# Softmax attention on one core: values projected for two groups of heads at once, and the loop over groups written out

## What is computed

```
xq = (x @ wq + bq).reshape(S, 16, 128)        # 16 query heads
xk = (x @ wk + bk).reshape(S, 4, 128)         # 4 groups share a key head ...
xv = (x @ wv + bv).reshape(S, 4, 128)         # ... and a value head
for group g, query head h in g (4 of them):
    attn = softmax(xq[:, h] / sqrt(128) @ xk[:, g].T)     # 1024 x 1024
    out[:, h] = attn @ xv[:, g]
x = x_in + out.reshape(S, 2048) @ wo + bo
```

## Time and profile before

| | before |
|---|---|
| median of three runs | 1137.98 us |
| the profiled execution, its own time | 1133.82 us |
| its span | 1132.0 us |
| mean granted TensorE clock | 0.974 |
| attention phase in it | from about 16 to 623 us |
| busy: TensorE, VectorE, ScalarE, GpSimd | 92%, 67%, 53%, 50% |

### The profile page before, as it was taken

The page is one execution under the profiler, slowest core; times in us unless marked ns, Lnnn a source line. Parts: engine busy times, 40 slices in busy tenths (PEclk is TensorE's granted clock), DMA queues, the critical chain, the costliest instruction groups (busy, mean ns, idle before and its releaser), DMA issues. The chain is left out here.

```text
span 1132.0 us, 18077 instructions
## 1 busy us (share of the span) xinstructions
PE 1045.5 (92%) x6180; PEld 879.3 (78%) x6180; DVE 763.1 (67%) x1344; ACT 599.5 (53%) x1059; POOL 562.3 (50%) x408
## 2 busy tenths in 40 slices
PE   5899999999999999999998989998888887999992
PEld 4788888888887888888887676664666586999992
DVE  4777764777566776657774654466687855788887
ACT  3566653666545666446662433342533235888881
POOL 1574623656335564335650256773324676755553
PEclk9999999999999999999999899999998898999996
DMA  7400440001800672000000236651300266777766
GB/s 198 52 29 1 53 41 3 19 11 33 61 2 2 223 215 84 1 1 1 1 1 1 77 98 208 209 195 56 107 1 5 100 211 214 237 236 234 233 218 212
DMA packets 45641, 109.92 MB, mean 97 GB/s; under 512 B 8519, under 2 KB 26069, under 8 KB 43504
## 3 DMA queue, kind: packets, MB, share of 16 engines
q1 hardware_dynamic: 38640, 95.46, 30.4%
q0 software_dynamic: 6912, 13.30, 3.1%
HBM read 94.27 MB, written 41.29 MB: 120 GB/s over the span
## 5 line engine op out<-in xcount | busy, mean ns | idle before, releaser
L422 POOL TENSOR_TENSOR at_prob<-at_prob,at_inv_sum 128x1024 f32<-128x1024 f32 x128 | 243.8, 1907 | 287.4 <-DVE at_inv_sum L647 287.4
L612 ACT ACTIVATE at_pt_h<-ps 128x512 fp32r<-128x512 f32 x256 | 139.1, 596 | 147.8 <-PE ps L537 147.7
L697 DVE TENSOR_TENSOR at_pt_l<-ps,at_pt_h 128x512 fp32r<-128x512 f32 x256 | 164.5, 684 | 60.6 <-ACT at_pt_h L612 60.5
L686 DVE TENSOR_REDUCE at_neg_max<-ps 128x1 f32<-128x1024 f32 x128 | 156.1, 1219 | 40.4 <-PE ps L41 40.0
L579 ACT ACTIVATE at_prob<-ps,at_neg_max 128x1024 f32<-128x1024 f32 x128 | 143.8, 1123 | 18.4 <-DVE at_neg_max L686 18.4
L537 PE MATMUL ps<-ident,at_prob 128*128 128x128 f32 x1024 | 133.0, 273 | 3.8 <-POOL at_prob L422 3.8
L537 PEld LDWEIGHTS ps<-ident,at_prob 128*128 128x128 f32 x1024 | 119.2, 140 | 20.9 <-POOL at_prob L422 4.7
L2079 POOL DMA_INDIRECT lines<-f_y,f_x_raw x96 | 96.3, 1003 | 71.8 <-ACT f_y L1995 43.7
L39 PE MATMUL ps<-at_k_h,at_q_h 128*128 128x512 f32 x256 | 108.9, 425 | 0.0
L41 PE MATMUL ps<-at_k_h,at_q_l 128*128 128x512 f32 x256 | 100.7, 393 | 0.0
L39 PE MATMUL ps<-at_pt_h,at_v_h 128*128 128x512 f32 x256 | 100.5, 392 | 0.0
(11 more groups left out here) (314 smaller groups left out, 2509.0 us busy)
## 6 DMA issues: line engine op xcount, KB each, us to landing
e_raw<-in_we SPq DMA_DIRECT2D x32, 624.0 KB, 4.1
f_cw_row<-cw SPq DMA_DIRECT2D x32, 512.0 KB, 4.4
slots<-in_empty SPq DMA_DIRECT2D x4, 3456.0 KB, 43.7
f_x_raw<-slots SPq DMA_DIRECT2D x32, 432.0 KB, 4.7
lines<-in_empty SPq DMA_DIRECT2D x3, 2048.0 KB, 32.5
f_e_raw<-in_we SPq DMA_DIRECT2D x32, 128.0 KB, 2.7
at_wq_raw<-in_wq SPq DMA_DIRECT2D x4, 512.0 KB, 3.3
at_wo_raw<-in_wo SPq DMA_DIRECT2D x4, 512.0 KB, 3.3
```

The costliest lines, as they stand in the source:

```text
L422: nc.gpsimd.tensor_tensor(prob[:, t % RING, :], prob[:, t % RING, :], inv_sum[:, t:t + 1].broadcast_to([P, T]), ALU.mult).then_inc(normed, 1)
L612: nc.scalar.activation(pt_h[:, e[1] % PT, :], turned(e[1]), ACT.Copy).then_inc(pt_high, 1)
L686: nc.vector.tensor_reduce(neg_max[:, t:t + 1], slot(n, start), AX.XY, ALU.max, negate=True).then_inc(maxed, 1)
L697: nc.vector.tensor_tensor(pt_l[:, e[1] % PT, :], turned(e[1]), pt_h[:, e[1] % PT, :].bitcast(F32), ALU.subtract).then_inc(pt_split, 1)
```

## The change

The values of two groups are projected together: one stationary token tile against the 256 columns of two value heads, in two jobs `("v", 0)` and `("v", 1)` of four token tiles each. This happens in the opening (groups 0 and 1) and in the change from group 1 to 2 (groups 2 and 3). `v_full`, `v_h` and `v_l` hold two groups. The split of the first group of a pair, `("vs", 0)`, is in the opening or within the change; that of the second, `("vs", 1)`, in the middle of the steady part of groups 0 and 2. The loop over groups is written out on every engine, with constants in place of registers. Keys' and values' weights have buffers, loads and splits of their own. The norm's centred input `xc` lies in the last two slots of `prob`, and its two small buffers are allocated last.

```diff
-    opening = [("k",), ("q", 0), ("v",)] + [("s", s) for s in range(LEAD)] + [("vs",)] + pair("t", 0)
-    steady = []
+    opening = [("k",), ("q", 0), ("v", 0), ("v", 1)] + [("s", s) for s in range(LEAD)] + [("vs", 0)] + pair("t", 0)
+    def steady(g):
+        events = []
...
+            if g % 2 == 0 and s == STEPS // 2:
+                events.append(("vs", 1))
...
-    change = [("k",)] + pair("p", at) + pair("t", at + 4) + [("v",)] + pair("p", at + 2) + pair("t", at + 6)
-    for n in range(3):
-        change += pair("s", 2 * n) + pair("p", at + 4 + 2 * n) + pair("t", at + 8 + 2 * n)
-    change += pair("s", 6) + pair("p", at + 10) + pair("s", 8) + pair("p", at + 12)
-    change += [("vs",)] + pair("s", 10) + [("y", 0)] + pair("t", 0) + [("y", 1)]
+    def change(g):
+        projects = (g + 1) % 2 == 0
+        events = [("k",)] + pair("p", at) + pair("t", at + 4) + [("v", 0)] * projects + pair("p", at + 2) + pair("t", at + 6)
+        events += [("v", 1)] * projects
+        for n in range(3):
+            events += pair("s", 2 * n) + pair("p", at + 4 + 2 * n) + pair("t", at + 8 + 2 * n)
+            events += [("vs", 0)] * (projects and n == 1)
+        events += pair("s", 6) + pair("p", at + 10) + pair("s", 8) + pair("p", at + 12)
+        return events + pair("s", 10) + [("y", 0)] + pair("t", 0) + [("y", 1)]
...
-        norm = Norm(nc, net, "n0", mem, load=True)
+        norm = Norm(nc, net, "n0", mem, load=True, xc=prob[:, RING - 2:, :].rearrange("p r (k d) -> p (r k) d", d=D))
...
             run(-1, opening, 0)
-            with eng.Fori(0, KV - 1) as g:
-                run(g, steady + change, first)
-            run(KV - 1, [e for e in steady if e != ("q", PER)] + closing, first)
+            start = first
+            for g in range(KV):
+                events = steady(g) + (change(g) if g < KV - 1 else closing)
+                run(g, events, start)
+                start += len(jobs_of(events))
...
-                            for i in range(TT):
-                                toks = slice(i * P, (i + 1) * P)
+                            for i in range(TT // 2):
+                                toks = slice((e[1] * TT // 2 + i) * P, (e[1] * TT // 2 + i + 1) * P)
                                 for c in range(DC):
-                                    last = product(nc, slot(n, start)[:, i // 4, (i % 4) * P:(i % 4 + 1) * P], xn_h[:, c, toks],
-                                                   xn_l[:, c, toks], wkv_h[:, 1, c, :], wkv_l[:, 1, c, :], c == 0, c == DC - 1)
+                                    last = product(nc, tokens_of(slot(n, start), i), xn_h[:, c, toks], xn_l[:, c, toks],
+                                                   wv_h[:, c, :], wv_l[:, c, :], c == 0, c == DC - 1)
...
-                            inverts(0 if start == 0 else 3)
-                            if start:
-                                dve.wait_ge(pv_done, LIFT + STEPS * (g + 1))
+                            if start == 0:
+                                inverts(0)
+                            k = e[1]
+                            if k and g:
+                                dve.wait_ge(pv_done, LIFT + STEPS * g)
```

More of the change, by code:

```diff
@@ L273, in jobs_of @@
         return [e for e in events if e[0] in "kvqy" or (e[0] == "s" and e[1] % 2 == 0)]
-    first, lap = len(jobs_of(opening)), len(jobs_of(steady + change))
-    assert lap % 2 == 0
+    first = len(jobs_of(opening))
     with ExitStack() as mem:
@@ L337, in proj_count, with v_high, v_split, keys_ready @@
             if e[0] == "k":
-                return 2 + PROJ * (g + 1) if not (isinstance(g, int) and g < 0) else 1
-            return 2 + PROJ * g + e[1] if not (isinstance(g, int) and g < 0) else 2
+                return 2 + PROJ * (g + 1) if g >= 0 else 1
+            return 2 + PROJ * g + e[1] if g >= 0 else 2
+        def v_high(k):
+            return v_parts, 2 * k + 1
+        def v_split(k):
+            return v_parts, 2 * k + 2
+        def keys_ready(g):
+            return (1, 3, 4, 6)[g]
+        def values_ready(g):
+            return (2, 5)[g // 2]
         def read_of(g, e, nxt):
@@ L345, in read_of @@
             if e[0] == "v":
-                return v_added, own + 1
+                return v_added, own + e[1] + 1
             if e[0] == "s":
@@ L382, in _ @@
                 sp.dma_start(bo[:, :], net.dram["bo"].partition_broadcast(P)).then_inc(consts, 16)
-                with sp.Fori(0, KV - 1) as g:
-                    sp.wait_ge(wo_split, 1 + 4 * g)
+                for g in range(KV - 1):
+                    if g:
+                        sp.wait_ge(wo_split, PER * g)
                     sp.dma_start(wo_raw[:, :, :], net.dram["wo"][g]).then_inc(wo_loaded, 16)
-                    sp.wait_ge(wkv_split, g + 1)
-                    load(g + 1, "kv")
+                    sp.wait_ge(wkv_split, keys_ready(g))
+                    load(g + 1, "k")
+                    if g % 2:
+                        sp.wait_ge(wkv_split, values_ready(g - 1))
+                        load(g + 1, "v")
                     sp.wait_ge(wq_split, 2 * (g + 1))
@@ L457, in _ @@
                         .then_inc(wq_split, 1)
+                pool.wait_ge(w_high, 2 + DC)
+                nc.gpsimd.tensor_tensor(wv_l[:, :, :], wv_raw[:, :, :], wv_h[:, :, :].bitcast(F32), ALU.subtract).then_inc(wkv_split, 1)
                 for t in range(LEAD // 2):
                     normalise(t + 1, t)
-                with pool.Fori(0, KV - 1) as g:
+                for g in range(KV - 1):
                     group(g, range(LEAD // 2, TILES + LEAD // 2))
@@ L466, in run @@
                 def run(g, events, start):
-                    jobs = jobs_of(events)
-                    spots = [n for n, e in enumerate(events) if e in jobs and (e[0] in "kvqy" or e[1] % 2 == 0)]
-                    before = jobs_of(steady + change)[-2:]
+                    spots = [n for n, e in enumerate(events) if jobs_of([e])]
                     n = start - 1
@@ L476, in begin @@
                             sem_, count = read_of(g, events[q], belongs_next(events, q))
[L477 removed]
+                        elif g > 0:
+                            sem_, count = read_of(g - 1, ("y", k), False)
+                        else:
                             return
[L479 to L482 removed]
                         pe.wait_ge(sem_, count)
[L485 to L492 removed]
+                    if g == 0:
+                        pe.wait_ge(exped, LEAD // 2)
                     for place, e in enumerate(events):
@@ L547, in run @@
                             keys = slice(kt * P, (kt + 1) * P)
-                            product(nc, o_bank(u), v_h[:, keys], v_l[:, keys], pt_h[:, e[1] % PT, :], pt_l[:, e[1] % PT, :],
+                            product(nc, o_bank(u), v_h[:, g % 2, keys], v_l[:, g % 2, keys], pt_h[:, e[1] % PT, :], pt_l[:, e[1] % PT, :],
                                     kt == 0, kt == KT - 1).then_inc(pv_done, 1)
@@ L564, in _ @@
                 norm.wait_parts(pe)
-                laps(pe, run)
+                laps(run)
                 bridge(nc, net, 4, 2)
@@ L590, in run @@
                             act.wait_ge(proj_full, count)
-                            if not (isinstance(g, int) and count == 1):
+                            if count > 1:
                                 act.wait_ge(proj_split, count - 1)
@@ L633, in _ @@
                 act.wait_ge(consts, 64)
-                laps(act, run)
+                laps(run)
             @block.vector
@@ L672, in run @@
[L672 to L680 removed]
+                            dve.wait_ge(values_full, own + e[1] + 1)
@@ new lines, in run @@
+                            part = slice(e[1] * BANK, (e[1] + 1) * BANK)
+                            nc.vector.tensor_tensor(v_full[:, :, part].rearrange("p g (i d) -> p i g d", d=DH),
+                                                    slot(n, start).rearrange("p n (i g d) -> p (n i) g d", g=2, d=DH),
+                                                    bv[:, own * DH:(own + 2) * DH].rearrange("p (g d) -> p g d", d=DH).unsqueeze(1)
+                                                    .broadcast_to([P, TT // 2, 2, DH]), ALU.add).then_inc(v_added, 1)
@@ L721, in _ @@
                 nc.vector.tensor_scalar(bq[:, :], bq[:, :], Q_SCALE, None, ALU.mult).then_inc(bq_scaled, 1)
-                laps(dve, run)
+                laps(run)
                 dve.wait_ge(y_added, LIFT + DC * KV)
```

132 lines of the change are left out of this document (63 added, 69 removed).

## The result

The changed kernel takes 1118.87 us (median of four runs, 1118.58 to 1119.49), the kernel before 1137.03 us beside it (four runs, 1133.95 to 1138.25): ratio 0.9858 [0.9842, 0.9874]. In a second series the changed kernel took 1122.21 us (six runs, 1117.71 to 1129.74) against 1136.82 (17 runs): 0.9899 [0.9856, 0.9942].

A forecast was written before the change was run, and what follows sets the result against it. Attention was taken to be bound by TensorE's stream, so time cut there comes off the total. From a median of 1138.0 us, +0.49 + 0.40 - 8.6 - 3.7 = -11.4 gave 1126.6 us, range 1121 to 1132.

The forecast's parts named there:

- Part 1, the values: Value projections shared by two groups: +0.49 us in the opening, +0.40 at change 1 to 2, -8.6 at the other two.
- Opening +0.49: In the opening, 48 value matmuls of 256 columns take 5.80 us instead of 5.31, all of it reaching the end.
- Rival D: Wide value matmuls take as long as their columns, so value work stays 21.6 us; 1136.5 us, no change; chance 0.03.
- The changes 0-1 and 2-3: Group changes left without value work: 5.40 us goes, 1.1 returns as a stall before the second transposes; 4.3 saved each.
- Part 2, the loop: Lap edges on TensorE: writing out the loop removes gaps of 1.95 and 1.72 us, -3.7 us.
- Rival B: Lap-edge gap stays, for VectorE's add or fetching of straight code; only the values' gain counts, -7.7, 1130.3 us; chance 0.06.
- Registers at 0: Register instructions for wait counts on TensorE's sequencer go, 3.4 us if none were hidden; taken as 0, about 1 for range.
- Part 3, the splits at 0: Value splits of 1.9 us on VectorE move to earlier places and fit by 0.2 to 0.9 us: 0.
- Rival C: VectorE is late after the moved splits and transposes wait: +5.7 us at most, 1132.3 us; chance 0.07.
- Part 4, loads and placement: Separate key and value weight loads, norm scratch in the probabilities' last slots, all attention buffers moved: 0.
- rival E: Moved buffers slow the 1536 score and product matmuls by 0.008 us each, 12 us, ending at 1139; chance 0.05.
- The sum: Whole change, all of it in attention: +0.49 + 0.40 - 8.6 - 3.7 = -11.4 us, giving 1126.6 us.

The follow-up runs named there:

- the two narrow kernels: Changed kernel with each value product cut into two of 128 columns, 1130.31 us; the same with the 2 MB fill issued ahead of the query load, 1129.67 us.

## Why the prediction came out as it did

**Part 1, the values: right.** Opening +0.49: from the first value matmul to tile 0 it was 7.34 us for 6.93, so +0.41. Matmuls of 256 columns at 0.12: yes, 5.75 us for 48; the two narrow kernels show that it is their number and not their columns that counts. Rival D is dead: cut in half, the same columns cost 4.9 us more. The changes 0-1 and 2-3 were to give 4.3 each, with 1.1 of 5.4 handed back to the second t t. They gave 4.5: scores started 3.17 us behind the first t t, not 3.3, and 0.9 was handed back.

**Part 2, the loop: right**, -3.7 forecast, -3.7 measured by the loop alone from tile 6 on (575.3 to 571.6). That the two agree so well is partly luck: the three changes lost both edges (3.67 us) and some 0.5 more, and got the new idle of 0.62 in return. Rival B is dead as far as the edge goes. Its second half, that straight code has to be fetched, may be that idle in the change 1-2 of the written-out kernel.

**Registers at 0: nearly.** The idle before the output projection is 0.60 us with the loop, 0.42 in the changed kernel; with the placement changed and the loop kept it is 0.6 still, with the loop written out 0.4. The change 2-3, which never had a taken branch, went from 49.41 to 49.27 us with the loop written out. Some 0.2 us in each of three changes, then; that it is the registers, and not something else about the loop, is argued.

**Part 3, the splits at 0: right**, maximum at 91.09 (forecast 91.1), `pt_l` from 92.21 (92.3) to 93.49, transposes at 93.91 without idle. Rival C is dead, but it was near: 2.34 us more at each of the three splits gave 5.4 in all.

**Part 4, loads and placement: this is the step that failed.** "I know no row that prices this" stood there, and I entered 0 and kept placement for rival E alone, as a loss. It was a gain, since the old place was the bad one: 2.5 us of the rest in the kernel before, 1.9 of it in the four middles, and 2.3 in the changed kernel. Rival E looked at the right matmuls, with the wrong sign and too large a size: 8 ns for each of the 1536, where the scores gained 2.1 and the products 0.3. I had the clue in hand. The distances of 0.234 and 0.226 were noted as not one number, with the address as a possible cause; what I left out is that a spread of that kind can be collected as well as lost.

**The sum.** Two of the runs lie on the way from one kernel to the other, so the rest can be followed step by step: 575.3 us before, 571.6 with the loop written out, 562.5 in the changed kernel at the old offset of 96 bytes, 560.2 in the changed kernel. That is loop -3.7, values -9.1 and placement -2.3, together -15.1; the forecast for the same stretch was -3.7, -8.2 (-8.6 + 0.4) and 0. Of the 0.9 by which the values gave more, 0.6 is the idle of 0.62 us, which the written-out kernel has and the changed one has not, and 0.3 the smaller stalls.

**The median.** Attention gave -14.8, the medians of the first series -18.2. The other 3.4 is not the change's: the second series gives -14.6, and the first four runs, within 1 us of each other, were a fortunate sample of a kernel that spreads from 1117.7 to 1129.7. So the 7.7 us between 1126.6 and 1118.87 are 3.4 of attention, 3.4 of such luck, and 0.9 by which the median before had come down. Either of the first two alone would have left the time at about 1122.2, inside the range; it took both to leave it. The forecast had said that 4.2 us of session belong in the range, but set its lower end at 1121 from a mechanism 3.4 us too small.

**Open:** why the offset matters, and which of a matmul's two operands it slows. The means by kind tell the matmuls apart, not the operands; buffers moved one at a time would tell, and that was not tried.

## What to carry to other kernels

Where a kernel is a stream of one engine for hundreds of microseconds, a change that adds or removes a small buffer ahead of its operands changes two things, and the second has a sign of its own: measure it with a pad, not with a guess. Merging small matmuls is priced by their number as long as the distance between starts hardly moves with the columns (here 0.11 us at 128, 0.12 at 256). And when work that covers something is removed, look for what is then late, put a number on it, and try the order in which independent work covers it again: here it was worth another 0.65 us per place in the attention phase, which the medians of whole runs could not yet show.

## What the runs showed of the hardware that was not expected

- The offset of the operands in a partition changes TensorE's stream: 97.80, 97.92, 98.62 and 98.29 us for the same 25 tiles at 0, 32, 64 and 96 bytes. At 96 the scores are slower (243.3 ns from start to start for 241.2), at 64 above all the products (230.4 for 227.6).
- A taken branch on TensorE's sequencer took 3480 and 3711 ns at the end of a lap of 150 us, with a 16 KB packet of the instruction queue inside each, and 222 and 240 ns at the end of a loop body of 25 us, without one.
- TensorE can stand idle in straight-line code with nothing to wait for: 0.62 and 1.14 us put down to "issue" while a 2 MB fill was under way. In one kernel the clock fell to its lower level behind the idle, and together it cost 2.8 us, gone when the fill was issued earlier.
- One phase took 151.5 to 157.1 us with the same instructions, by how long the granted clock stayed at the 1.2 GHz level: 3.4 us in the shortest, 17.1 in the longest.
